# Two-layer transformer kernel: the coordinate descent without its unread bf16 products

## The chip, the cores and the metric

The kernel runs as one program on one core of a Trainium2 chip. The metric is the device time of one execution in microseconds (us); lower is better. The engines of the core are named as the profile names them: PE is TensorE's matmul, PEld its weight load, DVE is VectorE, ACT is ScalarE, POOL is GpSimd and SP is SyncE.

## The reference, cut to what matters

The program is a stack of two layers over 2048 tokens of 128 channels: window attention with rotary positions, an MLP, a delta-rule attention, a second MLP, and at the end a feed-forward part that is routed. Each of the four parts is followed by a layer norm. The change lies in the routed part:

```
def coor_descent(s, n_iters, k, eps):
    logk = jnp.log(jnp.asarray(k, s.dtype))
    a0 = jnp.zeros_like(s[..., :1])
    b0 = -s
    def body(carry, _):
        a, b = carry
        a = eps * (logk - jax.nn.logsumexp((s + b) / eps, axis=-1, keepdims=True))
        b = -jax.nn.relu(s + a)
        return ((a, b), None)
    (a, b), _ = jax.lax.scan(body, (a0, b0), None, length=n_iters)
    return jnp.exp((s + a + b) / eps)

light_out = feedforward(x, gamma_l, w1_l, b1_l, w2_l, b2_l)
s = jnp.einsum('bnd,d->bn', x, routing_token)
scores = coor_descent(s, N_ITERS, effective_k, EPS)                  # 50 iterations
selected_scores, selected_indices = jax.lax.top_k(scores, NUM_HEAVY)  # 128 tokens
routed = jnp.take_along_axis(x, selected_indices[..., None], axis=1)
routed_out = feedforward(routed, gamma_h, w1_h, b1_h, w2_h, b2_h)
heavy_out = jnp.zeros_like(x).at[batch_range, selected_indices].set(routed_out)
return light_out + heavy_out
```

Every one of the 50 iterations needs a sum over all tokens from the iteration before. Both feed-forwards (a light one with 64 inner channels and a heavy one with 512) are independent of that loop until the selection.

## The kernel before, in words

All tokens stay in SBUF as 16 blocks of 128 tokens; four blocks make a group of 512 tokens. Every engine has a program of its own, written out in order, and the engines wait for each other on semaphores. Nothing is scheduled by a tool, so an engine does its instructions in the order in which the code lists them.

The parts follow each other: attention, first MLP, delta-rule attention, second MLP, then the descent (with the routed feed-forwards done in between), then the selection, the last layer norm and the store.

In the descent the sum over tokens runs as a ring between DVE and PE. DVE takes the minimum of each token's exponential with the current value and adds the results per partition into `partials` (L1214). PE multiplies them with a matrix of equal numbers (`inverse_k`, L902), which adds over the partitions and leaves the new value in PSUM bank 6 (named O in the profile). DVE reads it from there for the next minimum. There are 49 such turns, i = 0 to 48.

A search for the 128th largest score shares the ring: in each pair of turns DVE counts how many tokens reach three tried values (L1194), PE adds the counts over the partitions (L905, in odd turns, ahead of the turn's piece), and DVE picks a digit (L1179) and makes the next three values (L1188).

The routed feed-forwards are cut into 80 pieces of one or two matmuls (`ffn_piece`): L836 and L846 are the first matmuls of the light and the heavy one, L856 and L866 the second ones. `pieces_in(i)` gives turn i its pieces: none before turn 2, then about one a turn. ACT applies the gelu (L1456, L1461) and, in between, the exponentials (L1467) and logarithms (L1489) that the ring needs every seven turns. The last 20 pieces come behind the descent.

`warm(n, b)` (L877) issues n bf16 matmuls of a 128x128 matrix of ones (`ones_bf`) with itself into PSUM bank b (2 is named QK, 1 is S in the profile). Nothing reads their results. They stand ahead of the descent (L883 to L899) and in it: four in each of turns 0 to 3, behind that turn's L902 and L905 and ahead of its piece, and two in every even turn from turn 4 on, with a wait for `channels_kept` ahead of them (ACT's last copy out of bank 1).

Of the kernel before, what the change touches and what calls it, by code (L numbers as in the profile page):

```python
# [62 lines left out]
def build(nc, x, w_q, w_k, w_v, w_o, late_weights, row_vectors, kv_bias, out, late):  # L63
# [54 lines left out]
    FIRST_CARRYING = 2  # L118
# [4 lines left out]
    def pieces_in(i):  # L123

        total = PIECES_EACH * len(PIECES)
        carrying = DESCENT - 1 - FIRST_CARRYING
        start = lambda i: BEFORE_DESCENT + (total - BEHIND_DESCENT - BEFORE_DESCENT) * (i - FIRST_CARRYING) // carrying
        return range(start(i), start(i + 1)) if i >= FIRST_CARRYING else range(0)
# [16 lines left out]
    with ExitStack() as ctx:  # L145
# [365 lines left out]
        def _(pe):  # L511
# [361 lines left out]
            def ffn_pieces(ps):  # L873
                for p in ps:
                    ffn_piece(p)

            def warm(n, b=2):  # L877

                for _ in range(n):
                    nc.tensor.matmul(B[b][:, 0:P], ones_bf[:], ones_bf[:], start=True, stop=True)  # L880
# [19 lines left out]
            for i in range(DESCENT - 1):  # L900
                pe.wait_ge(partials_ready, i + 1)
                nc.tensor.matmul(B[6][:, 0:1], inverse_k[:], partials[:, 0:1], start=True, stop=True).then_inc(a_ps, 1)  # L902
                if i % 2 == 1:
                    pe.wait_ge(counts_ready, (i + 1) // 2)
                    nc.tensor.matmul(B[7][:, 0:DIGITS], ones_bf[:], counts[:], start=True, stop=True).then_inc(counts_ps, 1)  # L905
                if i < 2 * FIRST_CARRYING:
                    warm(4)
                elif i % 2 == 0:
                    pe.wait_ge(channels_kept, 5 * TG)
                    warm(2, 1)  # L910
                ffn_pieces(pieces_in(i))
            pe.wait_ge(counts_ready, ROUNDS)
            nc.tensor.matmul(B[7][:, 0:DIGITS], ones_bf[:], counts[:], start=True, stop=True).then_inc(counts_ps, 1)
# [783 lines left out]
```

## Time and profile before

| what | value |
|---|---|
| median of three runs | 486.85 us |
| the three runs | 480.68, 499.92, 486.85 us |
| the profiled execution | 479.4 us |
| its span, first to last instruction | 477.6 us |
| mean granted TensorE clock over the span | 0.959 |
| PE, busy share of the span | 85% |
| DVE | 65% |
| ACT | 54% |
| POOL | 37% |

The granted clock is the share of 2.4 GHz that TensorE was given: 1.00 is 2.4 GHz and 0.50 is 1.2 GHz. Matmul ends are modelled in the profile, so a busy time of PE contains the run-out of each matmul. An f32 matmul leaves two records, a bf16 matmul leaves one.

### The profile page before, as it was taken

What the parts mean: (1) busy time and instruction counts of PE and PEld (TensorE: products, weight loads), DVE (VectorE), ACT (ScalarE), POOL (GpSimd) and SP (SyncE); (2) the same over time, 40 slices, a digit from 0 to 9 for tenths busy, and PEclk for the clock granted to TensorE, in tenths of its full rate; (3) what the DMA queues carried; (4) which work ended last, traced back from release to release, by engine and by line L of the source; (5) the groups of instructions that cost most, each with busy time, mean ns of one, the idle gap of its engine ahead of it and who ended that gap; (6) DMA issues with size and microseconds to landing.
All of it is one profiled execution on the core that took longest, in us unless ns stands there. A gap on an engine that the chain in (4) does not pass through costs nothing.

```text
span 477.6 us, 18398 instructions
## 1 busy us (share of the span) xinstructions
PE 404.4 (85%) x7496; PEld 358.9 (75%) x7496; DVE 309.7 (65%) x1555; ACT 259.2 (54%) x654; POOL 174.6 (37%) x196
## 2 busy tenths in 40 slices
PE   2886999889998899988889985999996789889880
PEld 1775898879897799977757864998995477767670
DVE  1577876868768777767763679222035895888564
ACT  3244656556565565646473482346600448886937
POOL 2465433643454534543353557100005684000012
PEclk9997999989999999989999998899999799999986
DMA  6467365556666556656000000000000000000003
GB/s 231 114 144 179 83 155 124 125 147 152 159 159 160 146 134 157 179 130 149 19 2 0 1 0 3 4 4 3 0 1 1 0 2 1 1 3 2 0 2 88
DMA packets 20660, 35.38 MB, mean 74 GB/s; under 512 B 4512, under 2 KB 11680, under 8 KB 20576
## 3 DMA queue, kind: packets, MB, share of 16 engines
q1 hardware_dynamic: 20000, 33.16, 27.8%
q8 instruction: 60, 0.98, 0.9%
q10 hardware_dynamic: 576, 1.05, 0.6%
q14 instruction: 24, 0.20, 0.1%
HBM read 7.85 MB, written 1.05 MB: 19 GB/s over the span
## 4 chain that ended last, share of the span: by engine, by line
PE 60%; DVE 16%; ACT 7%; issue 6%; POOL 4%; SPq 3%; DMA 3%; ACTq 0%; POOLq 0%; DVEq 0%
PE QK L521 9%; PE VY L594 5%; PE O L572 4%; PE S L548 4%; PE PT L558 3%; PE O L663 3%; PE PT L581 3%; SPq L445 2%; PE S L740 2%; PE QK L721 2%; DVE unread_tests L1194 2%; PE S L735 2%; DMA t_swap<-t_sin 2%; POOL qk L1527 2%; PE S L756 2%
## 5 line engine op out<-in xcount | busy, mean ns | idle before, releaser
L1527 POOL TENSOR_TENSOR qk<-t_cos,t_swap 128x512 f32<-128x512 f32 x64 | 80.6, 1280 | 99.9 <-DMA t_swap<-t_sin 97.3
L1285 ACT ACTIVATE probs<-probs,negative_max 128x64 f32<-128x64 f32 x256 | 68.0, 338 | 44.0 <-DVE negative_max L952 43.1
L943 DVE TENSOR_TENSOR t_cos<-QK,cos 128x512 f32<-128x512 f32 x64 | 43.9, 685 | 32.0 <-PE QK L521 16.3
L1566 POOL TENSOR_TENSOR rstd<-var_eps,minus_half 128x4 f32<-128x4 f32 x24 | 25.4, 1057 | 100.3 <-DVE var_eps L996 95.6
L952 DVE CUSTOM_DVE_ANT_0 probs<-S,masks 128x64 f32<-128x64 f32 x256 | 39.4, 219 | 12.8 <-PE S L548 12.7
L943 DVE TENSOR_TENSOR t_sin<-QK,sin 128x512 f32<-128x512 f32 x64 | 43.5, 679 | 0.0
L521 PE MATMUL QK<-xnT,wq 128*128 128x128 f32 x256 | 36.8, 290 | 1.8 <-DVE t_sin L943 1.1
L1306 ACT COPY oT<-PT 128x512 f32<-128x512 f32 x32 | 18.7, 584 | 35.0 <-PE PT L581 34.9
L521 PEld LDWEIGHTS QK<-xnT,wq 128*128 128x128 f32 x256 | 33.6, 205 | 2.8 <-ACT xnT L1316 1.1
L594 PE MATMUL VY<-wo,oT 128*128 128x128 f32 x256 | 34.8, 280 | 0.7 <-ACT oT L1306 0.7
L572 PE MATMUL O<-v_before,probsT 64*32 64x65 f32 x1024 | 29.5, 229 | 7.0 <-issue 7.0
L521 PE MATMUL QK<-xnT,wk 128*128 128x128 f32 x256 | 35.1, 281 | 0.1
L572 PE MATMUL O<-v_own,probsT 64*32 64x65 f32 x1024 | 30.6, 230 | 3.3 <-issue 3.2
L521 PEld LDWEIGHTS QK<-xnT,wk 128*128 128x128 f32 x256 | 32.2, 197 | 0.6 <-DVE t_sin L943 0.6
L594 PEld LDWEIGHTS VY<-wo,oT 128*128 128x128 f32 x256 | 31.8, 195 | 1.0 <-ACT oT L1306 0.9
L548 PE MATMUL S<-qk 64*32 64x64 f32 x2048 | 28.2, 229 | 2.2 <-POOL qk L1527 2.2
L572 PEld LDWEIGHTS O<-v_before,probsT 64*32 64x32 f32 x1024 | 23.5, 106 | 7.3 <-issue 7.2
L548 PEld LDWEIGHTS S<-qk 64*32 64x32 f32 x2048 | 22.8, 108 | 7.0 <-POOL qk L1527 3.1
L1611 POOL TENSOR_TENSOR XC<-XA,delta_bias 128x512 f32<-128x512 f32 x4 | 5.0, 1270 | 63.0 <-DVE delta_bias L1116 63.0
L572 PEld LDWEIGHTS O<-v_own,probsT 64*32 64x32 f32 x1024 | 23.2, 106 | 5.0 <-issue 4.9
L1300 ACT COPY v_own<-VY 128x512 f32<-128x512 f32 x32 | 18.7, 586 | 12.2 <-PE VY L536 9.6
L581 PE MATMUL PT<-ident,o_sb 128*128 128x128 f32 x128 | 19.9, 279 | 6.0 <-ACT probsT L1292 6.0
(277 smaller groups left out, 1100.3 us busy)
## 6 DMA issues: line engine op xcount, KB each, us to landing
t_swap<-t_sin SPq DMA_DIRECT2D x124, 128.0 KB, 2.5
v_before<-v_own SPq DMA_DIRECT2D x32, 132.0 KB
v_before<-v_own SPq DMA_DIRECT2D x62, 66.0 KB
late_tile<-late_weights SPq DMA_DIRECT2D x7, 189.0 KB
x_sb<-x SPq DMA_DIRECT2D x4, 256.0 KB, 4.6
out<-XA SPq DMA_DIRECT2D x4, 256.0 KB, 2.3
cos<-rope_cos SPq DMA_DIRECT2D x3, 256.0 KB, 3.5
sin<-rope_sin SPq DMA_DIRECT2D x3, 256.0 KB, 4.6
```

The source lines that it names most:

```text
L521: last = nc.tensor.matmul(QK[j][:, m * P:(m + 1) * P], w[:, f], xnT[:, block_of(u)], start=True, stop=True)
L548: last = nc.tensor.matmul(S[WINDOW * i:WINDOW * i + WINDOW, e ^ (i // 2), m, :], qk[r, half(u), m, WINDOW * (i + 1):WINDOW * (i + 2)], qk[ ...
L572: last = nc.tensor.matmul(O_ps[WINDOW * i:WINDOW * i + WINDOW, e, m, 0:D + 1], probsT[r, half(u), m, WINDOW * i:WINDOW * i + WINDOW], v[:, ...
L581: last = nc.tensor.transpose(PT[:, m * P:(m + 1) * P], o_sb[:, half(u), m].rearrange("p e d -> p (e d)"), ident[:])
L594: last = nc.tensor.matmul(VY[:, 0:C], oT[:, n, :], wo[:, n, :], start=(m == 0), stop=(m == PAIRS - 1))
L943: last = nc.vector.tensor_tensor(dst[:, u % G, PAIRS * j:PAIRS * j + PAIRS], QK[j][:].rearrange("p (m t) -> p m t", m=PAIRS), table[:, tok ...
L952: last = nc.vector.tensor_tensor_reduce(out=probs[:, u % G, m, e, :], in0=S[:, e, m, :], in1=masks[:, min(u // G, 1), :], scale=-1.0, scal ...
L1285: last = nc.scalar.activation(probs[:, u % G, m, e, :], probs[:, u % G, m, e, :], ACT.Exp, scale=-1.0, bias=negative_max[:, u % G, e, m:m ...
L1300: nc.scalar.copy(v_own[:, b % V_SLOTS, :, PAIRS * h:PAIRS * h + PAIRS, 0:D], VY[:].rearrange("p (e m d) -> p e m d", e=2, m=PAIRS)).then_i ...
L1306: nc.scalar.copy(oT[:, PAIRS * (u % G):PAIRS * (u % G) + PAIRS, :], PT[:].rearrange("p (n q) -> p n q", n=PAIRS)).then_inc(oT_done, 1)
L1527: nc.gpsimd.tensor_tensor(qk[:, h, c, WINDOW:WINDOW + P], t_cos[:, h, c], t_swap[:, h, c], ALU.add).then_inc(rope_done, 1)
L1566: nc.gpsimd.tensor_tensor(rstd[:, grp(q)], var_eps[:, grp(q)], minus_half[:, grp(q)], ALU.pow).then_inc(roots_done, 1)
```

## The change

Inside the descent's loop on PE the products of `warm` are taken out, in turns 0 to 3 and in the even turns behind. The wait for `channels_kept` is kept once, at turn 4. The products ahead of the descent stay. No other engine's program is changed.

```
             if i % 2 == 1:
                 pe.wait_ge(counts_ready, (i + 1) // 2)
                 nc.tensor.matmul(B[7][:, 0:DIGITS], ones_bf[:], counts[:], start=True, stop=True).then_inc(counts_ps, 1)
-            if i < 2 * FIRST_CARRYING:
-                warm(4)
-            elif i % 2 == 0:
+            if i == 2 * FIRST_CARRYING:
                 pe.wait_ge(channels_kept, 5 * TG)
-                warm(2, 1)
             ffn_pieces(pieces_in(i))
```

`FIRST_CARRYING` is 2 and `TG` is 4. That is 4 x 4 + 23 x 2 = 62 matmuls fewer.

On PE, at the start of the descent (L902 is the ring's product, L905 that of the counts, L880 the product of `warm`):

```order
 L836 MATMUL VY<-xT,late_tile 64x256 x2
 L880 MATMUL QK<-ones_bf 128x128 x8
-L902 MATMUL O<-partials,inverse_k 128x1
-L880 MATMUL QK<-ones_bf 128x128 x4
-L902 MATMUL O<-partials,inverse_k 128x1
-L905 MATMUL O<-counts,ones_bf 128x3
-L880 MATMUL QK<-ones_bf 128x128 x4
-L902 MATMUL O<-partials,inverse_k 128x1
-L880 MATMUL QK<-ones_bf 128x128 x4
+L902 MATMUL O<-partials,inverse_k 128x1 x2
+L905 MATMUL O<-counts,ones_bf 128x3
+L902 MATMUL O<-partials,inverse_k 128x1
```

The eight products ahead of the first turn stay; the first turns now hold the ring's products alone.

On PE, at turn 4, with the semaphores that an instruction waits for:

```order
 L846 MATMUL QK<-xT,late_tile 128x256
 L902 MATMUL O<-partials,inverse_k 128x1 [waits partials_ready]
-L880 MATMUL S<-ones_bf 128x128 [waits channels_kept]
-L880 MATMUL S<-ones_bf 128x128
+L846 MATMUL PT<-xT,late_tile 128x256 [waits heavy_hidden_kept,channels_kept]
```

The wait moves from the removed product to the piece behind it; all later even turns lose two products in the same way and have no such wait any more.

## Rows read from the trace of the kernel before

**Rows 1.** The granted clock in the page's 40 slices, in tenths.

```profile
PEclk9997999989999999989999998899999799999986
```

**Rows 2.** Instructions of lines 880, 902: minimum/median/maximum ns, first and last start.

```profile
L880 PE MATMUL QK<-ones_bf x126: 216/219/230, 384.2 to 404.6; 128*128 128x128 bf16 x126
...
L880 PE MATMUL S<-ones_bf x46: 216/217/218, 405.3 to 447.7; 128*128 128x128 bf16 x46
...
L902 PE MATMUL O<-partials,inverse_k x98: 167/250/271, 401.8 to 447.5; 128*128 128x1 f32 x98
```

**Rows 3.** Chain that ended last, 401 to 450: start, us, what.

```profile
403.06 0.24 PE QK L880 x4
403.52 0.24 PE QK L880 x4
...
404.56 0.24 PE QK L880 x4
...
405.76 0.46 DVE unread_tests L1194 x6
406.45 0.54 PE PT L846 x2
...
444.70 1.28 ACT L1467
```

**Rows 4.** Timeline of one pair of turns: start, us, engine, line, operation.

```profile
408.65 0.28 PE L902 MATMUL O<-partials,inverse_k 128*128 128x1 f32 x2
...
408.79 0.27 PE L880 MATMUL S<-ones_bf 128*128 128x128 bf16 x2
...
408.90 0.65 PE L846 MATMUL PT<-xT,late_tile 128*128 128x256 f32 x2
...
409.26 0.32 PEld L902 LDWEIGHTS O<-partials,inverse_k 128*128 128x128 f32 x2
...
409.39 0.28 PE L902 MATMUL O<-partials,inverse_k 128*128 128x1 f32 x2
...
409.70 0.23 DVE L1214 TENSOR_SCALAR_CACHE_REDUCE unread_minima<-exp_scores,O 128x16 f32<-128x16 f32 x1
...
409.79 0.18 PE L905 MATMUL O<-counts,ones_bf 128*128 128x3 bf16 x1
...
409.83 0.68 PE L846 MATMUL PT<-xT,late_tile 128*128 128x256 f32 x2
...
410.34 0.28 PE L902 MATMUL O<-partials,inverse_k 128*128 128x1 f32 x2
```

**Rows 5.** Line 880 alone in the descent: us, PE and PEld busy, clock, DMA share, GB/s.

```profile
401.80:448.30 46.50, 7.91 (x65) 5.88 (x62) 1.00 0.01 2
```

**Rows 6.** Stretches: us, PE, PEld, DVE, ACT, POOL busy, clock, DMA share, GB/s.

```profile
401.80:448.30 46.50, 41.62 (x320) 34.10 (x317) 39.70 (x376) 37.58 (x49) 0.00 (x0) 1.00 0.01 2
206.80:210.10 3.30, 3.30 (x18) 3.30 (x17) 0.76 (x2) 1.54 (x5) 0.00 (x0) 0.50 0.72 165
292.10:295.50 3.40, 3.02 (x42) 2.50 (x39) 3.37 (x4) 0.37 (x1) 2.10 (x2) 0.50 0.02 5
455.90:459.30 3.40, 3.40 (x18) 3.23 (x16) 1.99 (x10) 2.44 (x8) 0.00 (x0) 0.51 0.00 0
```

**Rows 7.** PE's timeline at idle stretches; in brackets the idle time before, and its releaser.

```profile
161.51 0.44 PE L558 MATMUL PT<-ident,probs 128*128 128x128 f32 x2 [1.67 <-issue]
161.78 1.06 PE L594 MATMUL VY<-wo,oT 128*128 128x128 f32 x8
...
206.67 1.82 PE L594 MATMUL VY<-wo,oT 128*128 128x128 f32 x8
...
291.65 0.32 PE L693 MATMUL O<-keys_T 128*64 128x128 f32 x1 [1.69 <-ACT keys_T L1370]
...
426.87 0.70 PE L846 MATMUL QK<-xT,late_tile 128*128 128x256 f32 x2 [0.50 <-ACT hid L1461]
...
454.68 0.40 PE L922 MATMUL VY<-tie,before 128*128 128x16 f32 x2 [1.96 <-DVE tie_totals L1258]
```

## The prediction

> **What bounds the kernel now.** I read the clock in the page's slices first, to find the stretch and its clock; then the instructions of the line that goes; then the chain of waits through the descent, for what is on the path; then one pair of turns on the timeline; last, stretches in which the clock was low, for what such a stretch costs.
>
> The slices show a clock at or near full in all of the descent, about slices 34 to 38 of 40 [rows 1]. The row of the last 46 gives 217 ns each, and 16 of the 126 in the other row belong to the descent too [rows 2]; the ring's own records run from 401.8 to 447.5 us. In 46.5 us they make 7.91 us of PE's busy time (65 records: three of the eight ahead of the descent fall into that stretch) [rows 5], out of 41.62 us of PE in all, and the clock is 1.00 over the whole of it [rows 6]. So nearly a fifth of PE's busy time in the descent is theirs. But busy time counts each record's run-out; two of them delay the next matmul by 0.11 us, from 408.79 to 408.90 [rows 4].
>
> The chain shows whose time the descent is: DVE's counts, then the piece behind the count's product on PE, then the ring, with ACT's table loads toward the end (444.70, 1.28 us) [rows 3]. Of the 62 products it holds three groups of four, at 403.06, 403.52 and 404.56, 0.24 us each [rows 3]; none from turn 4 on is in the rows of the chain.
>
> **The change part by part.**
>
> *Sixteen products in turns 0 to 3.* By the chain, 3 x 0.24 = 0.72 us are on the path; the group in turn 0 is not. At 403.06 and 403.52 DVE is nearly as late as PE, so I take 0.24 (turn 3, ahead of a piece) and half of the other two: 0.5 us gained. Bounds: 0.24 and 0.72.
>
> *Forty-six products in the even turns from turn 4.* Take turn 8 [rows 4]. The ring's product starts at 408.65, the two products at 408.79, the piece at 408.90, the next ring product at 409.39. Its weight load started at 409.26, when DVE had delivered; so PE was late by 0.13 us, and two products fewer would let it start up to 0.11 us earlier. That gain goes nowhere: the next DVE minimum starts at 409.70 only because the counts stand ahead of it in DVE's order, and the product of the counts at 409.79 waits for those counts. The even half has slack, the odd half sets the pair's 1.69 us (408.65 to 410.34). I take 0. Bounds: 0, and 23 x 0.11 = 2.5 us if each were on the path. Their cover is DVE's count, which does not change.
>
> *The wait for the last copy out of bank 1.* It now stands once, on turn 4's piece, where a removed product waited for it before. That product started at 405.3, the first of its row [rows 2], and it was not held there for long enough to show in the chain: 0. Behind it in PE's queue stand the piece and the next ring product; both stood behind the same wait before.
>
> *What may come instead: the clock.* This is the only large term, and the trace of before does not show the descent without the products. What a low stretch costs can be read. Eight matmuls of line 594 take 1.06 us at the full clock and 1.82 us in the stretch behind 206.67 [rows 7], where the clock was 0.50 [rows 6], so a 128-column f32 record takes 0.11 us longer (0.76 / 7). A piece is four such records, or two of twice the columns: +0.43 us. In the odd half all of it is on the path: the pair goes from 1.69 to 2.12 us at least. In the even half the slack is from the end of the ring product (409.39 + 0.28) to 409.79, 0.12 us, plus the 0.11 that goes; so 0.2 us of the second 0.43 comes on top, and something for slower ring products: about 2.4 us a pair. The low stretches in the rows are 3.3 to 3.4 us [rows 6]. In 3.4 us at 2.4 us a pair 1.42 pairs are done, at the full clock 2.01: 0.59 pairs, or 1.0 us lost. Bounds for one low stretch: 0.7 us (3.4 x 0.43 / 2.12) and 1.7 us (all work at half speed). Where ACT sets the pace, at the table loads behind 444, it could also cost 0.
>
> How often? The rows speak both ways. Against a fall: before the clock fell at 292 and at 456, PE had stood idle for 1.69 and 1.96 us in one piece, and after 1.67 us of idleness at 161.5 it did not fall; in the descent the longest idle piece is 0.50 us (at 426.87) [rows 7]. For it: PE loses a fifth of its busy time in all of the 46.5 us at once [rows 5, 6], and the descent is made of pieces with short waits between them. The thinnest places are those where it waits already or where a piece is light: about 412, 421, 426 and 440 us. I take two falls of these four: +2.0 us. Bounds: none and seven (low in every second stretch of 3.4 us of the descent's 46.5), 0 to +7 us at 1.0 us each.
>
> The Trainium skill, page "TensorE: Matmul & The Clock Gate", has two rules that differ here. "Why this matters for your kernels" warns of long idle gaps between bursts of matmuls alone; by it the descent would stay at the full clock and the sum would be -0.5 us. "A second HAM failure mode: psum-queue depth-cycling" has the clock go to and fro when PE idles briefly and often between groups of matmuls; by it the sum would be positive. The rows agree with the first as far as they go (1.69 and 1.96 us against 0.50) and show no case for the second, since no stretch before the change is as thin for as long.
>
> *Sum.* -0.5 + 0 + 0 + 2.0 = +1.5 us on the profiled execution: 479.4 + 1.5 = 480.9 us. That execution was 7.45 us below the median of the three runs and the fastest of four; the four are 479.4, 480.68, 486.85 and 499.92, with their middle at 483.8. I take that as where a median of new runs lies: 483.8 + 1.5 = **485.3 us**.
>
> **The rivals.**
>
> *The clock holds.* Then only the direct gain is left, 0.24 to 0.72 us, at the outermost 62 x 0.055 = 3.4 us. Time: 483.8 - 0.5 = 483.3 us. For it speak the short idle pieces of the descent; against it, that a fifth of PE's busy time goes in one place.
>
> *The clock falls and stays low (the other side).* If PE at 1.2 GHz is not brought back by the descent's own pieces, all pairs run at about 2.4 us instead of 1.69: 24 x 0.7 = +17 us, less 0.5: 483.8 + 16.5 = 500.3 us, 3.4% over the forecast's base. Place: L846 and L866 pieces behind L902 and L905. It decides from the point where a low stretch is not over after 3.4 us but goes on for more than ten pairs (10 x 0.7 = 7 us, with two or three single falls besides). Against it: at the low clock the same pieces fill PE more (3.02 and 3.40 us of 3.40 in the last two low stretches), and the clock came back after each of these [rows 6].
>
> *Low in every second stretch.* The bound above: 483.8 + 7 - 0.5 = 490.3 us; still inside 2%.
>
> **How the numbers follow.** What this kernel's measurement can tell from no change is about 2%, or 9.7 us of 486.85. Chances: some falls, one to four, 0.55 (forecast, 485.3); the clock holds, 0.29 (483.3); low in every second stretch, 0.06 (490.3); stays low, 0.05 (500.3); 0.05 are left for the spread of the runs themselves, which was 19 us over three. The first three stay within 2%. Slower by over 2%: 0.05 + 0.03 of the spread = 0.08, and some of the alternating case on top of a slow median, 0.02: 0.10. Faster by over 2%: no step reaches 9.7 us (all 62 products on the path would give 3.4), so 0.02 for the spread alone. Same: 0.88. The range begins at the fastest execution with the direct gain alone, 479.4 - 0.5 = 479, and ends at the median run with four falls at their upper price, 486.85 + 6.8 - 0.5 = 493. It leaves out the case that stays low and the outer spread.
>
> **What would show it.** In the profile after: line 880 has 110 records, none behind the first ring product. The stretch from the first ring product to the last (401.8 to 447.5 us) is 45.7 us long now [rows 2]; the forecast wants 47 to 48 us with one or more rows of the clock at 0.50 in it, the first rival wants 45 to 45.5 us at 1.00. A pair at 1.00 should last the same 1.7 us as before, with the ring product of the even half starting with its weight load and not 0.13 us behind it; if pairs at 1.00 became shorter by 0.1 us, the slack in the even half was misread. In a low stretch a pair should last 2.1 to 2.5 us. The step most likely to fail is the count of falls: the trace of before holds no stretch like it.

## The result, and the profile after

The changed kernel takes 499.1 us (median of four executions, 497.53 to 500.31); the kernel before, on the same chip, 492.88 us (four executions, 480.68 to 499.92). The comparison leaves out executions more than 1.5% above a kernel's fastest; by it the changed kernel is slower by a ratio of 1.0333, with a 95% interval of 1.0267 to 1.0398. Two of the four executions of the kernel before, 498.92 and 499.92 us, lasted as long as the changed kernel's. The forecast was 485.3 us in a range of 479 to 493; the time is that of the rival in which the clock falls and stays low, worked out as 500.3 us.

The profiled execution takes 500.31 us, with a span of 498.5 us against 477.6, and a mean clock of 0.900 against 0.959. Of the 20.9 us more in the span, 1.1 lie ahead of the first ring product (402.9 against 401.8 us), 17.4 in the descent (402.86 to 465.98 is 63.1 us, against 45.8) and 2.4 behind it (32.5 against 30.1). The clock in the page's slices answers to [rows 1]:

```profile
PEclk9998999999999999999999988999998975555587
```

It is halved from the 34th slice to the 38th. The instructions of line 880 and of the ring's line answer to [rows 2] (minimum/median/maximum ns, first and last start):

```profile
L880 PE MATMUL QK<-ones_bf x110: 219/219/230, 385.3 to 402.8; 128*128 128x128 bf16 x110
...
L902 PEld LDWEIGHTS O<-partials,inverse_k x98: 186/333/338, 402.8 to 466.0; 128*128 128x128 f32 x98
L902 PE MATMUL O<-partials,inverse_k x98: 211/352/373, 402.9 to 466.1; 128*128 128x1 f32 x98
```

The 62 products are gone, none stands behind the first ring product. The ring's products slowed from a median of 250 to 352 ns. By stretches (us, then PE, PEld, DVE, ACT and POOL busy, clock, DMA share, GB/s), which answers to [rows 6]:

```profile
402.80:405.80 3.00, 2.37 (x17) 1.83 (x15) 2.43 (x26) 2.71 (x5) 0.00 (x0) 1.00 0.00 0
405.80:466.00 60.20, 60.20 (x241) 52.32 (x240) 36.53 (x345) 35.12 (x43) 0.00 (x0) 0.50 0.00 1
466.00:474.10 8.10, 8.10 (x34) 6.77 (x32) 2.94 (x24) 5.64 (x7) 0.00 (x0) 0.50 0.01 2
474.10:480.90 6.80, 4.29 (x35) 3.95 (x35) 4.58 (x17) 3.24 (x11) 1.02 (x1) 1.00 0.00 1
```

The first three turns run at 1.00; from 405.8 us on the clock is 0.50, and it stays there for 68 us, through all that is left of the descent and 8 us behind it. What PE did before it fell: the first turns, with no product and no piece in turns 0 and 1, and in them single idle pieces no longer than 0.34 us. In the 10.8 us before the fall no idle piece is above 0.35 us; one of 1.45 us ends where these begin, at 395.01, and the clock held behind it (in brackets the idle time before, and its releaser):

```profile
395.01 0.66 PE L644 MATMUL S<-ident,XB 128*128 128x128 f32 x4 [1.45 <-ACT XB L1388]
...
402.86 0.33 PE L902 MATMUL O<-partials,inverse_k 128*128 128x1 f32 x2
403.52 0.38 PE L902 MATMUL O<-partials,inverse_k 128*128 128x1 f32 x2 [0.34 <-DVE unread_minima L1211]
```

The next is one pair of turns at 0.50 (start, us, engine, line), the answer to [rows 4]:

```profile
411.42 0.42 PE L902 MATMUL O<-partials,inverse_k 128*128 128x1 f32 x2
...
411.70 1.20 PE L846 MATMUL PT<-xT,late_tile 128*128 128x256 f32 x2
411.88 0.23 DVE L1211 TENSOR_SCALAR_CACHE_REDUCE unread_minima<-exp_scores,O 128x16 f32<-128x16 f32 x1 [0.66 <-PE O L902]
...
412.27 0.76 PEld L902 LDWEIGHTS O<-partials,inverse_k 128*128 128x128 f32 x2
...
412.70 0.42 PE L902 MATMUL O<-partials,inverse_k 128*128 128x1 f32 x2
...
412.98 0.17 PE L905 MATMUL O<-counts,ones_bf 128*128 128x3 bf16 x1
...
413.01 1.20 PE L846 MATMUL PT<-xT,late_tile 128*128 128x256 f32 x2
...
414.00 0.42 PE L902 MATMUL O<-partials,inverse_k 128*128 128x1 f32 x2
```

The pair lasts 2.58 us (411.42 to 414.00), against 1.69. Both halves are now PE's: from a piece's start to the next ring product 0.99 to 1.00 us, from a ring product to what stands behind it 0.28 us. The product of the counts at 412.98 no longer waits for the counts; DVE waits for the ring, 0.66 us here. In sum over the descent (waiting instruction, who ended the wait, us in total, times, longest), before:

```profile
PEld O L905 <- DVE unread_tests L1194: 5.0, 21, 0.5
...
DVE unread_minima L1214 <- PE O L902: 3.3, 13, 0.5
```

and after:

```profile
DVE unread_minima L1211 <- PE O L902: 17.1, 32, 0.9
...
PEld O L902 <- DVE unread_minima L1211: 4.1, 9, 0.8
```

The wait for DVE's counts is down to 0.4 us in sum, and DVE's wait for PE grew from 3.3 to 17.1 us: the bound of the descent went from DVE to PE.

### The profile page after: what moved, and what is told of

It reads as the page before. It is cut to its first block, busy times and chain, and to the rows that moved or that the text cites. A ratio compares the mean times of both kernels' runs of the same rounds, so it can differ in the third digit from the quotient of the medians.

```text
span 498.5 us, 18275 instructions
## 1 busy us (share of the span) xinstructions
PE 424.3 (85%) x7434; PEld 377.8 (76%) x7434; DVE 308.6 (62%) x1555; ACT 259.5 (52%) x654; POOL 175.1 (35%) x196
## 4 chain that ended last, share of the span: by engine, by line
PE 59%; DVE 12%; SPq 10%; issue 6%; ACT 5%; POOL 4%; DMA 3%; ACTq 0%; POOLq 0%; DVEq 0%
PE QK L521 6%; PE QK L866 5%; SPq L445 5%; PE VY L594 4%; PE O L572 3%; PE O L663 3%; PE S L548 3%; PE PT L846 3%; PE O L902 3%; PE QK L846 3%; PE PT L558 2%; PE S L740 2%; PE PT L581 2%; PE QK L721 2%; PE S L735 2%
## 5 line engine op out<-in xcount | busy, mean ns | idle before, releaser
L902 PEld LDWEIGHTS O<-partials,inverse_k 128*128 128x128 f32 x98 | 27.9, 318 | 8.5 <-DVE unread_minima L1211 4.1
L572 PE MATMUL O<-v_own,probsT 64*32 64x65 f32 x1024 | 30.1, 229 | 3.6 <-issue 3.6
L866 PE MATMUL QK<-late_tile,hid 128*128 128x128 f32 x128 | 30.5, 402 | 0.0
```

Source lines behind the costliest of these rows:

```text
L572: last = nc.tensor.matmul(O_ps[WINDOW * i:WINDOW * i + WINDOW, e, m, 0:D + 1], probsT[r, half(u), m, WINDOW * i:WINDOW * i + WINDOW], v[:, ...
L866: last = nc.tensor.matmul(B[2][:, tok(i)], hid[:, j, tok(GB * q + i)], W["w_h2"][:, tok(j)], start=(j == 0), stop=(j == NHF - 1))
```

## The experiments

Theory A: the thin first turns made the clock fall, and a descent that is at 1.00 holds it by its pieces. Theory B: the even turns need their products too. All edits are shown against the changed kernel, cut to the lines that matter; an omission inside is marked with three dots. "Clock" of an execution is its mean granted clock.

**Only the products of turns 0 to 3 put back.**

```
+                if i < 2 * FIRST_CARRYING:
+                    warm(4)
```

> The 16 products of turns 0 to 3 are put back, the 46 of the even turns stay out. Theory A (the fall at 405.8 came from the thin first turns, and a descent that is once at 1.00 holds it by its pieces): clock 1.00 through the descent, mean clock about 0.96, 480 to 487 us. Theory B (the even turns need their products too): the clock falls later, at one of the thin places (412 to 441), and stays at 0.50 from there to the end of the descent: 488 to 498 us, mean clock 0.90 to 0.94.

Four executions: 489.94, 493.72, 497.76 and 502.08 us, at a clock of 0.930, 0.910, 0.911 and 0.901. Three are in the range of theory B, one is above it. The profiled one is the first:

```profile
403.30:433.70 30.40, 26.83 (x185) 21.70 (x182) 25.52 (x244) 26.17 (x34) 0.00 (x0) 1.00 0.01 2
433.80:455.10 21.30, 21.30 (x88) 18.67 (x89) 13.49 (x125) 11.31 (x15) 0.00 (x0) 0.50 0.00 0
```

The clock holds through the start and falls at 433.8 us, behind the two light pieces of line 856 and the turn around them; it then stays low to the end of the descent. That is theory B. The stretch at 1.00 also shows what the even products cost while the clock holds. The next rows are a pair of turns with none of them, from the timeline of PE and its weight loads:

```profile
425.79 0.28 PE L902 MATMUL O<-partials,inverse_k 128*128 128x1 f32 x2
425.93 0.68 PE L846 MATMUL PT<-xT,late_tile 128*128 128x256 f32 x2
...
426.41 0.30 PEld L902 LDWEIGHTS O<-partials,inverse_k 128*128 128x128 f32 x2 [0.20 <-DVE unread_minima L1213]
426.45 0.34 PE L902 MATMUL O<-partials,inverse_k 128*128 128x1 f32 x2
...
426.93 0.10 PEld L905 LDWEIGHTS O<-counts,ones_bf 128*128 128x128 bf16 x1 [0.23 <-DVE unread_tests L1193]
...
426.97 0.68 PE L846 MATMUL PT<-xT,late_tile 128*128 128x256 f32 x2
...
427.49 0.28 PE L902 MATMUL O<-partials,inverse_k 128*128 128x1 f32 x2
```

1.70 us (425.79 to 427.49), the 1.69 us of [rows 4]. The piece starts 0.14 us behind the ring product, not 0.25, and nothing is won by it, since line 905 waits for the counts (0.23 us). The ring product of the even half now starts 0.04 us behind its weight load instead of 0.13, as the forecast wanted. While the clock holds, the products are free.

**Only the products of the even turns put back.**

```
-                if i == 2 * FIRST_CARRYING:
+                if i >= 2 * FIRST_CARRYING and i % 2 == 0:
                     pe.wait_ge(channels_kept, 5 * TG)
+                    warm(2, 1)
```

> The 46 products of the even turns are put back, the 16 of turns 0 to 3 stay out. Theory A: the clock falls at the start as in the changed kernel, and since the low pairs hold it low, it stays: 497 to 503 us, mean clock 0.90. Theory B, in the form that the even products alone hold the clock: 480 to 487 us, clock 1.00 in the descent. If the even products bring a fallen clock back: a low stretch of some us at 405, then 1.00, and 483 to 490 us.

486.72, 487.41, 492.96 and 499.07 us, at 0.949, 0.949, 0.915 and 0.903; no single outcome. The last is the profiled one:

```profile
401.30:404.30 3.00, 2.36 (x17) 1.81 (x15) 2.50 (x26) 2.63 (x5) 0.00 (x0) 1.00 0.00 0
404.40:467.50 63.10, 63.10 (x284) 54.61 (x283) 36.37 (x343) 35.12 (x43) 0.00 (x0) 0.50 0.00 1
```

Without the first sixteen the clock can fall at the start, and two products a pair did not bring it back in 63 us here. At the low clock they cost time: the descent lasts 66.2 us, against 63.1 without them. In two of four executions the descent lost little, by their clocks; no trace of these was kept. So neither half of what was removed holds the clock by itself in every execution.

**A burst in the middle.**

```
+                if i == 16:
+                    warm(80, 1)
```

> The changed kernel with 80 unread bf16 products in one piece at turn 16. They cost 4.5 to 8.5 us on the path. Both theories: the clock is 0.50 from about 406 and comes back to 1.00 within the burst. Theory A (once up, the pieces hold it): 1.00 from there to the end of the descent, 16 pairs at 1.7 instead of 2.6 us, so 500 - 14 + 4 to 8 = 490 to 494 us. Theory B: it falls again at a thin place behind the burst and stays low: 500 to 507 us.

502.55 (profiled) and 495.21 us, at 0.915 and 0.916.

```profile
406.00:408.80 2.80, 2.16 (x17) 1.63 (x14) 2.31 (x24) 2.69 (x5) 0.00 (x0) 1.00 0.00 0
408.80:426.20 17.40, 17.40 (x71) 15.63 (x71) 10.05 (x97) 11.07 (x13) 0.00 (x0) 0.50 0.00 1
429.30:449.70 20.40, 18.24 (x152) 15.14 (x151) 14.22 (x132) 13.03 (x16) 0.00 (x0) 1.00 0.01 2
449.80:467.80 18.00, 18.00 (x73) 15.31 (x73) 11.19 (x108) 9.31 (x12) 0.00 (x0) 0.50 0.01 1
```

The burst (426.23 to 432.3 us, 6.1 us on the path) brings the clock back while it runs. It is 1.00 for 20.4 us, 17.4 of them in the bare descent behind the burst, and then it falls again; theory B again.

**Four products in the odd turns' idle time.** The first question left: does more of the same hold the clock in every execution, and at what cost? The four stand between the ring's product and the wait for the counts; turns 0 to 3 are as before, and the even turns have none.

```
+                if i == 2 * FIRST_CARRYING + 1:
+                    pe.wait_ge(channels_kept, 5 * TG)
                 if i % 2 == 1:
+                    if i > 2 * FIRST_CARRYING:
+                        warm(4, 1)
                     pe.wait_ge(counts_ready, (i + 1) // 2)
...
-                if i == 2 * FIRST_CARRYING:
-                    pe.wait_ge(channels_kept, 5 * TG)
+                if i < 2 * FIRST_CARRYING:
+                    warm(4)
```

> As before in turns 0 to 3; from turn 5 on four products stand in each odd turn between the ring's product and the wait for the counts, where PE idles, in place of two in each even turn behind it. Four take 0.22 us at 1.00, the idle time there is 0.3 us, so a pair stays at 1.70 us. If the clock is what counts: 1.00 in the descent in every run, mean clock 0.955 or more, 479 to 485 us, and no run near 499 as two of the four of the kernel before. If the products only do harm where they stand: 485 us and more at the same clock.

Ten executions, 478.70 to 485.12 us, median 482.98, all at 0.953 to 0.967. Thirteen of the kernel before on the same chip lie between 478.99 and 502.32 us, median 491.51, at 0.903 to 0.970. Against the four of these up to 481.61 us, all at 0.949 or above, the ratio is 1.005 (0.998 to 1.012): no gain over an execution that kept its clock. The descent of the profiled one, and a turn of it:

```profile
405.80:451.70 45.90, 43.51 (x360) 35.95 (x358) 38.91 (x369) 36.83 (x47) 0.00 (x0) 1.00 0.01 2
```

```profile
413.33 0.34 PE L902 MATMUL O<-partials,inverse_k 128*128 128x1 f32 x2
413.53 0.38 PE L880 MATMUL S<-ones_bf 128*128 128x128 bf16 x4
413.81 0.18 PE L909 MATMUL O<-counts,ones_bf 128*128 128x3 bf16 x1
```

The four fit between 413.53 and the counts' product at 413.81. From the first to the last ring product it takes 45.9 us, against 45.8 in the profile of before.

**Number or place?** Four in the even turns, where the two stood, and two in the odd turns, with the rest as in the run with four there:

```
-                if i == 2 * FIRST_CARRYING:
+                if i < 2 * FIRST_CARRYING:
+                    warm(4)
+                elif i % 2 == 0:
                     pe.wait_ge(channels_kept, 5 * TG)
+                    warm(4, 1)
```

> As the kernel before, with four products instead of two in each even turn. If the number of products decides whether the clock holds: every run at a mean clock of 0.953 or more, as with the four in the odd turns, 479 to 487 us, with pairs at 1.00 up to 0.1 us longer than 1.69 where the even half has no slack left. If the place decides (the idle time of the odd turns): part of the runs between 490 and 502 us at 0.90 to 0.93.

```
+                    if i > 2 * FIRST_CARRYING:
+                        warm(2, 1)
```

> Two products in each odd turn ahead of the wait for the counts, none in the even turns: the number of the kernel before at the other place. If the number decides: as the kernel before, part of the runs at 478 to 482 us and part up to 502 us with the clock down to 0.90. If the place decides: every run 478 to 485 us at 0.953 or more.

Four in the even turns: 476.30, 478.58, 481.18 and 481.95 us, at 0.960 to 0.963. Two in the odd turns: 485.13 to 496.78 us, at 0.926 to 0.930. Their profiled descents, first the four, then the two:

```profile
404.10:450.00 45.90, 43.39 (x360) 36.72 (x357) 38.55 (x368) 36.85 (x47) 0.00 (x0) 1.00 0.01 2
```

```profile
409.20:439.70 30.50, 28.55 (x213) 22.45 (x210) 25.52 (x245) 26.23 (x34) 0.00 (x0) 1.00 0.01 2
439.80:462.50 22.70, 22.70 (x104) 20.03 (x104) 13.72 (x125) 11.19 (x15) 0.00 (x0) 0.50 0.00 1
```

Four hold the clock at either place, and two hold it in every execution at neither. Three in the even turns:

```
...
+                elif i % 2 == 0:
                     pe.wait_ge(channels_kept, 5 * TG)
+                    warm(3, 1)
```

> Three products in each even turn, four in turns 0 to 3: between the kernel before (two) and the run with four. If the number decides gradually: fewer falls than with two, part of the runs at 484 to 492 us and most at 477 to 483 us. If three are enough: all runs 476 to 483 us at 0.955 or more.

Ten executions, 481.51 to 493.48 us, at 0.927 to 0.963, median 489.21. Half of them are at 0.953 or above. The profiled one (490.78 us, 0.933):

```profile
403.50:434.00 30.50, 28.27 (x227) 23.62 (x224) 25.67 (x244) 26.16 (x34) 0.00 (x0) 1.00 0.01 2
...
434.60:455.00 20.40, 20.40 (x103) 17.96 (x102) 11.60 (x111) 9.70 (x14) 0.00 (x0) 0.51 0.00 1
```

It falls behind the two light pieces of line 856, at the same place as the two other profiled executions with a filled start and a fall (at 433.8 us with no later products, at 439.7 us with two in the odd turns), and three products a pair did not bring it back for 20 us. That place was not on the forecast's list of thin places. The place alone does not decide: in the run with the burst the clock was still 1.00 behind the same two pieces and fell 2.5 us later. On that chip three do not hold the clock in every execution; that the odds go up gradually with the number is not shown, since fourteen executions of the kernel before beside them had a median of 486.13 us.

**The same instructions without the columns.** The kernel before, each of its 62 products narrowed to one column:

```
+                for _ in range(n):
+                    nc.tensor.matmul(B[b][:, 0:1], ones_bf[:], ones_bf[:, 0:1], start=True, stop=True)
```

> The kernel before with its 62 products narrowed to one column: as many matmuls and weight loads as before at the same places, hardly any streaming. If the streaming of columns holds the clock: as the changed kernel, 496 to 502 us at 0.90. If the number of matmul instructions or the weight loads hold it: as the kernel before, part of the runs at 478 to 482 us.

496.53 to 501.56 us in four executions, at 0.887 to 0.898.

```profile
399.10:402.10 3.00, 2.59 (x33) 2.16 (x31) 2.47 (x26) 2.69 (x5) 0.00 (x0) 1.00 0.02 5
402.20:463.40 61.20, 61.20 (x284) 53.38 (x283) 36.39 (x343) 35.13 (x43) 0.00 (x0) 0.50 0.00 1
```

As many matmuls and weight loads as before at the same places, and the time of the changed kernel; the lowest of 51 executions of the kernel before is at 0.899. What held the clock were the columns that PE streamed, or the time that PE spent on them, which this run cannot tell apart; not the number of instructions or of weight loads.

**The thin start with four in each even turn.**

```
-                if i == 2 * FIRST_CARRYING:
+                if i >= 2 * FIRST_CARRYING and i % 2 == 0:
                     pe.wait_ge(channels_kept, 5 * TG)
+                    warm(4, 1)
```

> Four products in each even turn from turn 4, none in turns 0 to 3: the thin start of the changed kernel with the larger number behind it. If the number that keeps a clock at 1.00 also brings a fallen one back: a low stretch of 3 to 10 us at the start, 1.00 from there on, 480 to 486 us at 0.945 or more. If keeping and bringing back are two things (a low descent stays low): 0.50 from the start to the end of the descent, pairs of 2.8 us, 500 to 506 us at 0.90.

485.29 to 493.11 us in four executions, at 0.934 to 0.950. The profiled one (492.97 us, 0.945):

```profile
409.50:412.80 3.30, 2.66 (x20) 2.08 (x18) 2.79 (x27) 2.62 (x5) 0.00 (x0) 1.00 0.00 0
412.90:416.20 3.30, 3.30 (x19) 2.94 (x17) 1.70 (x19) 1.17 (x2) 0.00 (x0) 0.50 0.02 7
416.30:423.00 6.70, 6.48 (x51) 5.48 (x52) 5.74 (x56) 6.58 (x9) 0.00 (x0) 1.00 0.00 0
423.10:426.40 3.30, 3.30 (x20) 3.30 (x20) 1.73 (x19) 3.05 (x4) 0.00 (x0) 0.50 0.00 0
426.50:457.90 31.40, 29.43 (x239) 24.56 (x238) 26.26 (x250) 23.17 (x30) 0.00 (x0) 1.00 0.01 2
```

It falls at the start, and it comes back twice, each time after about 3.4 us. With four a pair the falls of this trace are short; this is the case that the forecast took for the changed kernel. The descent lasts 48.4 us, 2.6 more than before, for two such falls: 1.3 us each, where the forecast had put 1.0 with bounds of 0.7 and 1.7. The whole time is further above 480 than that: the first ring product starts at 409.45 us, 7.7 us later than in the profile of before, and 33.3 us follow the last one instead of 30.1. One of the four executions is inside the 480 to 486 us expected of short falls. Why the stretch ahead was longer was not followed up. In the thirteen profiled executions the first ring product starts between 399.15 and 409.45 us, with the same program up to there.

**Versions that hold the clock.** All products in idle time (four in turn 0, six in turns 1 and 3, four in each later odd turn), and that start with four in each even turn from turn 4:

```
                 if i % 2 == 1:
+                    warm(*((6,) if i < 2 * FIRST_CARRYING else (4, 1)))
                     pe.wait_ge(counts_ready, (i + 1) // 2)
...
+                if i == 0:
+                    warm(4)
```

> Four products in turn 0, six in turns 1 and 3 and four in each later odd turn, all ahead of the wait for the counts; none ahead of a piece. If the clock is what counts and PE's idle time hides them: 1.00 in the descent, every run 478 to 485 us at 0.953 or more, and the first two pairs 0.2 to 0.4 us shorter than the 1.39 and 1.99 us of the kernel before. If the thin turn 2 is enough for a fall: clock falls near 405 to 409 in part of the runs and these take 497 to 502 us.

```
+                    if i < 2 * FIRST_CARRYING:
+                        warm(6)
...
-                if i == 2 * FIRST_CARRYING:
+                if i == 0:
+                    warm(4)
+                elif i >= 2 * FIRST_CARRYING and i % 2 == 0:
                     pe.wait_ge(channels_kept, 5 * TG)
+                    warm(4, 1)
```

> The version that the runs point to: four products in turn 0 and six in turns 1 and 3 where PE waits for the counts, four in each even turn from turn 4. If four a pair hold the clock: every run between 476 and 485 us at 0.953 or more, against a kernel before whose runs lie between 479 and 502 us; against those runs of it in which the clock held as well, no difference beyond 0.5%. If the clock falls here too: runs of 489 us and more at 0.94 or less.

The first: 477.88 to 482.23 us in four executions, at 0.956 to 0.967, with the first pair of turns at 1.38 us and the second at 1.88, so that 0.1 us was won there and not 0.2 to 0.4 a pair. The second: twelve executions, 479.13 to 487.51 us, median 484.58, at 0.948 to 0.970; two are under the 0.953 that was expected of all, and five above the 485 us; seventeen of the kernel before beside them: 479.40 to 506.19, median 488.35, at 0.905 to 0.967. Against the seven of these up to 485.2 us, all at 0.953 or above, the ratio is 1.001 (0.9956 to 1.0064): nothing is won over an execution in which the clock held anyway. What these versions win over the kernel before, they win in the executions in which its clock falls.

Over the 117 executions with a recorded clock the time follows the clock, whichever kernel it is:

| mean granted clock | executions | median us | lowest to highest |
|---|---|---|---|
| 0.960 and over | 34 | 481.0 | 476.3 to 486.1 |
| 0.953 to under 0.960 | 17 | 485.1 | 479.3 to 489.8 |
| 0.945 to under 0.953 | 12 | 487.0 | 481.6 to 493.0 |
| 0.930 to under 0.945 | 19 | 489.9 | 484.9 to 495.2 |
| 0.905 to under 0.930 | 22 | 496.7 | 485.1 to 506.2 |
| under 0.905 | 13 | 499.8 | 496.5 to 502.1 |

Within a row the times still spread by 6 to 21 us, so the clock is not all of it; the 10 us by which the start of the descent varies are of that size. Of 51 executions of the kernel before beside these runs 18 are at 0.953 or above and 16 below 0.930; all 30 of the four versions with four products a pair and a filled start are at 0.948 or above, 476.3 to 487.5 us.

## Why the prediction was wrong

*What was right.* The mechanism (the clock falls, and that is the only large term), the sign, and the price of the rival that came true: 500.3 us worked out, 499.1 measured. The direct terms: the forecast took 0 for the 46 products of the even turns, and a pair without them at 1.00 takes 1.70 us against 1.69. For the sixteen it took 0.5 us with bounds of 0.24 and 0.72; the first pair is 1.39 us with and without them, the second 1.99 with and 1.80 in the thin start with four behind it, so 0.2 us, just below the bounds: the chain of waits named three groups of four, of which about one was really on the path. The moved wait cost nothing that shows. That 500.3 lies so close to 499.1 is luck in part: its 24 pairs at 0.7 us are a price too low and a count too high, as shown below, and of the 20.9 us between the two profiled executions 3.5 lie outside the descent, where the sum had nothing.

*The step that failed* is "How often?": two falls at thin places, each over after some 3.4 us. There was one fall, at a place that was not on the list of four (the start, whose sixteen products I had looked at only as a direct cost), and it lasted 68 us. The argument for short falls was, in the rival that came true, that "at the low clock the same pieces fill PE more (3.02 and 3.40 us of 3.40 in the last two low stretches), and the clock came back after each of these". PE's busy column reads 60.20 of 60.20 us in the low descent as well, and the clock did not come back. So that column does not tell whether the clock comes back. The low stretch of before behind 455.9 us held matmuls of one line in unbroken sequence (first row below); in the descent's pair 0.28 us pass from the start of each ring product to what stands behind it. The burst brought the clock back while it ran, and with four products a pair it came back by itself, so what PE does in a low descent decides whether it ends; the forecast took its length from stretches of another kind. What such a stretch must hold is not shown: behind the descent of the changed kernel, sequences of 8 matmuls ran at 0.50, 8 us in all, before the clock came back (the other rows).

```profile
455.32 4.11 PE L866 MATMUL QK<-late_tile,hid 128*128 128x128 f32 x20
...
468.25 2.08 PE L856 MATMUL S<-late_tile,light 64*128 64x128 f32 x8
470.26 2.07 PE L866 MATMUL QK<-late_tile,hid 128*128 128x128 f32 x8
```

The forecast itself named the count of falls as the step most likely to fail.

The second error is in the evidence for the rival's chance of 0.05. The four times of before, 479.4, 480.68, 486.85 and 499.92, were put down to "the spread of the runs themselves". No clock was recorded for the last three of them. Of the 51 executions of the kernel before with a recorded clock, the eleven of 497 us and more are all at 0.910 or below, and the ten under 482 us at 0.949 or above. So the 499.92 us was in all likelihood the mechanism at work: with two products a pair the clock falls in part of the executions, and without them it was low in all four. That the clock of before falls in the descent is inferred from its mean; no trace of such an execution was kept. A trace of one execution at 0.959 could not show it, but a spread of 19 us was a sign to look at the clock of each execution. About 10 us of such a spread arise ahead of the descent, as the starts of its first ring product show.

*The price.* The pair at 0.50 was worked out as 2.4 us and lasts 2.58. From a piece's start to the next ring product it is 0.99 and 1.00 us against 0.49 and 0.51 [rows 4], 0.5 us more where the rows of line 594 had given 0.43; and from a ring product to what stands behind it 0.28 us, against 0.14 at 1.00 with nothing between. The ring's own weight loads went from a median of 190 to 333 ns, which the sum had as "something for slower ring products"; before, they were

```profile
L902 PEld LDWEIGHTS O<-partials,inverse_k x98: 186/190/192, 401.7 to 447.5; 128*128 128x128 f32 x98
```

At 0.9 us a pair for the 22 pairs from turn 4 on that would be 19.8 us; the descent grew by 17.4, because nine of these pairs last 1.9 us and longer in the kernel before already and lost 0.68 us on average.

The Trainium skill, page "TensorE: Matmul & The Clock Gate", section "Why this matters for your kernels", warns of long idle gaps alone; here the clock fell with no idle piece above 0.35 us in the 10.8 us before, and it had held behind one of 1.45 us, so the measurement goes against a reading of that rule as the only case. Its section "A second HAM failure mode: psum-queue depth-cycling", by which brief idle times between groups of matmuls suffice, agrees with the trace as to the fall; it has the clock go to and fro, which the run with four products a pair behind a thin start shows (two low stretches of 3.4 us), while in the changed kernel it stayed at 0.50 for 68 us.

*Left open:* what decides, for the same program, in which execution the clock falls. No run here tells it, and the two executions of the run with the even products alone that kept a mean clock of 0.949 left no trace to compare.

## What to carry to other kernels

A ring of small matmuls between two engines can have two speeds: at 1.00 DVE set the pace and PE had idle time to fill, at 0.50 PE set it and its work did not lift the clock. The low one lasted to the end of the descent; without products the high one lasted 17 us behind a burst and 30 us behind a filled start. Products that nobody reads cost nothing where the engine waits anyway and the clock holds, so judge them by the clock's rows over several executions, not by the chain of waits of one. When one program's times spread by 4%, look at the granted clock of each execution before calling it noise.

## What was not expected of the hardware

The fall came with no idle piece of PE above 0.35 us in the 10.8 us before it, while 1.45 us in one piece ahead of these in the same execution, and 1.67 us in one piece, at 161.5 us in the profile of before, brought none [rows 7]. The low state lasted 68.3 us with PE's busy column at 100%. Of two programs with the same number of matmuls and weight loads, the one with 128 columns in its unread products was at a mean clock of 0.953 or more in 18 of 51 executions, the one with a single column at 0.898 or less in all four.
